# Cutting the beginning of a one-core attention block by batch and by query tile

## The chip, the core and the metric

The kernel runs on one core of a Trainium2 chip. The metric is device time in microseconds (us) of that core. Below, PE is the matrix engine (TensorE), DVE the vector engine, ACT the scalar engine, POOL the GpSimd engine and SP the engine that issues most DMAs. Each engine takes its instructions strictly in the order of its program; they meet only through semaphores.

## The reference

`x` is 2 batches of 256 tokens of 512 numbers, `ctx` 2 x 512 tokens of 128, everything float32. Three blocks follow each other, each with a residual and a layer norm:

```python
def bitnet_linear(x, weight, scale):
    s = max(mean(abs(weight), axis=1), 1e-8)
    return nan_to_num(einsum('bsi,oi->bso', x, sign(weight / s)) * (s * scale))
# 1: q = bitnet_linear(x, wq) (32 heads of 16), k, v = bitnet_linear(x, wk), (x, wv) (8 heads of 16)
#    softmax(q k / 4) v, then bitnet_linear(.., wo);       x = layernorm(x + ..)
# 2: cross attention of x on ctx, 512 keys, with an additive mask;  x = layernorm(x + ..)
# 3: y = x @ w_low.T + bias, w_low looked up in a table of 16 from 4 bit planes; x = layernorm(x + y)
```

So before the first score can be formed, the signs of the key and query weights must be multiplied with x, the absolute sums of the weights must be known, and the products scaled.

## The kernel before

**Units.** Attention is cut into 32 units: 16 of block 1 (2 batches x 8 key heads, 4 query heads each), 16 of block 2. A unit of block 1 has two key tiles (k = 0, 1), and each (unit, key tile) is a "chunk", numbered c = 2u + k. For each unit PE first forms the scores in bf16 three-part form (`scores`, L1138/L1141, into PA), DVE takes the row maxima (`maxima`, L911/L915), POOL splits these in three bf16 parts (`split_maxima`, L532 to L535), PE turns them into rows (`turn_maxima`, L1155), ACT copies the rows into QA (`rows`, L668). Only then can PE form the transposed scores with the maxima subtracted (`direct`, L1171, into PT), ACT take the exponential (`exps`, L656), and PE multiply by the values (`product`, L1199, into PO). ACT empties PO (`unload`, L675), PE turns it (`turn_unit`, L1225), DVE divides (`normalise`, L929, L934).

**Order.** All of it is written by hand. PE runs `scores` three units ahead of `direct`; `turn_maxima(u + 2)` stands at the end of chunk (u, 1), so `direct` of unit u + 1 stands behind it. `product(u)` waits for `rows(u + 2)`. POOL runs a loop over units: `split_maxima(u)`, and in units 1 to 8 two steps each of a side job `split_context` (L538 to L566): the sum of the output weights' absolute values (2 steps, in unit 1), parts of the context (8), V2 (2), and four products of the output weights with their scales `so` (2 in unit 7, 2 in unit 8). DVE has its own side job `weights` (one step in each chunk: splits of late query tiles, then bit masks and clamps, later merges), and a burst `output_scales` (L759 to L856) that forms `so`.

**Beginning.** SP loads wkv, x, wq whole, in this order. Then PE projects keys (`L1088`), queries of batch 0 (4 tiles), V (4 token tiles, L1111) and queries of batch 1 (4 tiles, L1097); a "tile" is 128 output columns. ACT scales each out of PSUM twice (L645, L646), DVE forms the bf16 parts (`split_q`, three instructions L769 to L771 behind a guard copy L800 that tests a limit read by `reg_load`), and SP spreads each part over partitions by six DMAs (`send_k`, `send_q`) into KA1 and QA, where `scores` reads them. The pairs ld_*, q_ready, q_out, q_split, qa_ready, ka1_ready are the semaphores of these steps; `signs` counts ACT's sign and absolute value of weights, `scales` DVE's scales.

**Idle products.** PE runs 28 products of constants at the start (L1084) and 28 before the last feed-forward (L1207); nothing reads them.

## Time and profile before

| | us |
|---|---|
| median of 3 runs (lowest, highest) | 313.03 (311.41, 313.76) |
| the profiled execution: its own time | 316.26 |
| the profiled execution: span of its trace | 313.5 |
| PE busy, of the span | 280.6 (89%) |
| DVE busy | 233.5 (74%) |
| ACT busy | 184.0 (59%) |
| POOL busy | 179.4 (57%) |

The span is what the trace covers; the execution's own time is 2.8 us more and lies around it. Busy time is a mean over very different stages: in the first 45 us of this program projections, splits and DMAs run, then 16 units of block 1 until about 117 us, then block 2.

### The profile page before, as it was taken

The page shows a single profiled execution, that of the slowest core. Times are in us where ns is not written, and L with a number is a line of the kernel's source. Part 1 is how long each engine was busy: PE and PEld are TensorE (multiplying, and loading weights), DVE is VectorE, ACT ScalarE, POOL GpSimd, SP SyncE. Part 2 cuts the span into 40 slices and gives each one's busy share as a digit, 9 for nine tenths or more (in the row PEclk, how much of TensorE's full clock was granted, in tenths as well). Part 3 has the DMA queues.
Part 4 walks back from the last instruction along what each step waited for, and adds up shares of the span by engine and source line. Part 5 has one row for each costly group of instructions (what it writes and reads, how often), then busy time and mean ns, then how long its engine had stood idle before and what let it go on. Part 6 is the DMA issues. An engine that isn't in the chain of part 4 may idle for free.

```text
span 313.5 us, 6246 instructions
## 1 busy us (share of the span) xinstructions
PE 280.6 (89%) x2176; PEld 176.1 (56%) x2176; DVE 233.5 (74%) x646; ACT 184.0 (59%) x325; POOL 179.4 (57%) x276
## 2 busy tenths in 40 slices
PE   7989879869898877899999899999999989999990
PEld 7679544434443332246556565666666656566880
DVE  2766377989748795997488977889899964773646
ACT  2236456867954689436456588777776754367010
POOL 8000077857975099787264897999998764320000
PEclk9979956998997997879999999999999999999997
DMA  7939942669910007600000008500000000001001
GB/s 231 365 106 124 134 45 48 90 95 205 121 53 2 0 12 125 69 2 0 4 0 2 0 17 126 64 1 2 3 0 2 1 2 0 0 36 37 0 1 67
DMA packets 15457, 17.16 MB, mean 55 GB/s; under 512 B 2112, under 2 KB 11456, under 8 KB 15424
## 3 DMA queue, kind: packets, MB, share of 16 engines
q1 hardware_dynamic: 14464, 16.29, 28.5%
...
q14 instruction: 16, 0.13, 0.2%
...
## 4 chain that ended last, share of the span: by engine, by line
PE 68%; DVE 15%; ACT 9%; issue 3%; DMA 3%; SPq 0%; POOL 0%; DVEq 0%; ACTq 0%
PE PT L1183 17%; PE PO L1199 14%; PE PA L1138 8%; DMA SM<-in_wq_T 3%; PE PT L1097 3%; PE PT L1171 3%; DVE mx L915 3%; PE PS L1237 3%; PE PA L1141 3%; ACT PTs L656 3%; PE PS L1241 2%; PE PS L1269 2%; ACT QA L668 2%; PE PT L1207 2%; PE PS L1281 2%
## 5 line engine op out<-in xcount | busy, mean ns | idle before, releaser
L656 ACT ACTIVATE PTs<-PT 128x512 f32<-128x512 f32 x192 | 110.7, 597 | 48.1 <-PE PT L1183 34.4
L596 POOL TENSOR_SCALAR SM<-SM,mx 128x512 f32<-128x512 f32 x128 | 97.3, 773 | 41.3 <-DVE mx L911 40.0
L911 DVE CUSTOM_DVE_ANT_0 SM<-PA,maskq 128x512 f32<-128x512 f32 x128 | 84.9, 685 | 20.2 <-PE PA L1138 19.9
L1183 PE MATMUL PT<-ident,SM 128*128 128x128 f32 x512 | 78.6, 278 | 2.1 <-ACT PTs L656 1.7
L1183 PEld LDWEIGHTS PT<-ident,SM 128*128 128x128 f32 x512 | 59.6, 141 | 26.2 <-issue 10.6
L1199 PE MATMUL PO<-PTs,V 128*32 128x256 f32 x768 | 54.1, 400 | 3.5 <-ACT QA L668 3.3
L1138 PE MATMUL PA<-KA,QA 96*128 96x512 bf16 x128 | 49.9, 398 | 4.7 <-DVE mx L911 4.3
L915 DVE TENSOR_REDUCE mx<-PA 128x2 f32<-128x512 f32 x64 | 40.9, 681 | 16.3 <-PE PA L1141 15.8
L1199 PEld LDWEIGHTS PO<-PTs,V 128*32 128x32 f32 x768 | 21.0, 112 | 26.2 <-issue 10.5
L532 POOL CAST SM<-mx 128x8 bf16<-128x8 f32 x16 | 5.3, 334 | 50.0 <-DVE mx L915 50.0
L1171 PE MATMUL PT<-QA,KA 99*128 99x512 bf16 x64 | 28.4, 443 | 2.5 <-ACT QA L668 1.4
L1141 PE MATMUL PA<-KA,QA 96*128 96x256 bf16 x128 | 26.6, 302 | 3.8 <-DVE mx L915 3.6
L675 ACT ACTIVATE wkvT<-PO 128x256 f32<-128x256 f32 x32 | 12.3, 384 | 24.0 <-PE PO L1199 23.9
L668 ACT ACTIVATE QA<-PO 3x512 bf16<-3x512 bf16 x32 | 18.8, 586 | 8.9 <-PE PO L1155 7.8
L1141 PEld LDWEIGHTS PA<-KA,QA 96*128 96x128 bf16 x128 | 13.0, 107 | 18.0 <-DVE mx L915 7.3
L1138 PEld LDWEIGHTS PA<-KA,QA 96*128 96x128 bf16 x128 | 12.7, 100 | 9.8 <-DVE mx L911 8.2
L583 POOL TENSOR_SCALAR wqT<-wqT,clamp_high,clamp_low 128x512 f32<-128x512 f32 x18 | 14.7, 819 | 0.8
L929 DVE RECIPROCAL rsum<-PM 128x8 f32<-128x8 f32 x32 | 6.4, 199 | 10.8 <-PE PM L1225 10.8
L1171 PEld LDWEIGHTS PT<-QA,KA 99*128 99x128 bf16 x64 | 6.7, 104 | 13.6 <-issue 7.3
L1225 PE MATMUL PM<-ident,wkvT 128*128 128x128 f32 x64 | 12.8, 282 | 0.5 <-ACT wkvT L675 0.5
L1097 PE MATMUL PT<-xT,wqT 128*128 128x256 f32 x48 | 12.7, 425 | 0.5 <-ACT wqT L632 0.5
L1097 PEld LDWEIGHTS PT<-xT,wqT 128*128 128x128 f32 x48 | 10.1, 214 | 2.3 <-ACT wqT L632 0.6
...
## 6 DMA issues: line engine op xcount, KB each, us to landing
...
```

What stands on the lines that cost most here:

```text
L583: nc.gpsimd.tensor_scalar(row, row, clamp_high[:, o, n:n + 1], clamp_low[:, o, n:n + 1], ALU.min, ALU.max).then_inc(leaf_ready, 1)
L596: nc.gpsimd.tensor_scalar(row, row, -1.0, mx[:, u % MX_RING, n:n + 1], ALU.mult, ALU.add).then_inc(sub_done, 1)
L656: nc.scalar.activation(PTs[:, c % PT_RING, j * 512:(j + 1) * 512], PT[:, (2 * c + j) % T_RING, :], ACT.Exp, scale=-1.0 if layer(u) else 1. ...
L668: nc.scalar.activation(QA[KR:KRM, b, heads.start + 2 * j:heads.start + 2 * j + 2, g * R // HT, :], maxima_rows[j], ACT.Copy).then_inc(rows ...
L911: vec.tensor_tensor_reduce(SM[:, u % SM_RING, n, :], PA[:, f % A_RING, :], maskq[:, n % QT, :], 1.0, LOWEST, ALU.add, ALU.max, mx[:, u % M ...
L915: vec.tensor_reduce(mx[:, u % MX_RING, QT * i:QT * (i + 1)], PA[:, f % A_RING, :].rearrange("p (q k) -> p q k", q=QT), AX.X, ALU.max).then ...
L1097: last = mm(q_psum(b, o), wqT[:, i, o * P:(o + 1) * P], xT[:, i, b * S:(b + 1) * S], start=(i == 0), stop=(i == DT - 1))
L1138: last = mm(PA[:, f % A_RING, :], QA[0:KR, b, h % HT, h // HT, q * P:(q + 1) * P], KA2[0:KR, g, b * T2:(b + 1) * T2], start=True, stop=True)
L1141: last = mm(PA[:, f % A_RING, q * S:(q + 1) * S], QA[0:KR, b, (g * R + i) % HT, g * R // HT, q * P:(q + 1) * P], KA1[0:KR, g, b * S:(b + 1 ...
L1171: mm(PT[:, n % T_RING, :], KA1[0:KRM, g, b * S + k * P:b * S + (k + 1) * P], QA[0:KRM, b, g * R % HT + 2 * j:g * R % HT + 2 * j + 2, g * R ...
L1183: last = nc.tensor.transpose(PT[:, n % T_RING, (i % 4) * P:(i % 4 + 1) * P], SM[:, u % SM_RING, i, k * P:(k + 1) * P], ident[:])
L1199: last = mm(PO[VW * r:VW * (r + 1), 0:S], V[:, batch(u) * key_tiles(u) + k, group(u), :], PTs[:, c % PT_RING, r * S:(r + 1) * S], start=(k ...
```

## The change

The beginning is cut finer. SP loads the first batch of x, the first quarter of wq, the second batch, the rest of wq. Keys are projected per batch; query tile (0, 0) and the keys of batch 0 are scaled, split and sent first, the tile by ACT's own DMA queue, under a limit of their own (`first_fits`). Of V, only the tiles of batch 0 stand in the beginning, behind `scores(0)`; the other two, and the query tiles (1, 2) and (1, 3), are computed by PE in the chunks 1, 2 and 4 to 7 (`later`). ACT takes the absolute value of the output weights in chunk (0, 0) and unloads the two late query tiles in chunk (4, 0). DVE's `output_scales` goes from unit 4 to unit 6, PE's sum of the output weights from unit 3 to unit 5. DVE's side job has three more steps (14 in place of 11), the split of the second batch's keys first and the split of the last two query tiles behind the clamps. Idle products go from 28 and 28 to 17 and 18. POOL's program is the same but for the counts it waits for.

```diff
-WARM = (28, 28)
+WARM = (17, 18)
...
-        OT = wkvT[:, 0, :]
+        OT = tmp2[:, 0:S]
...
+        Q_BANKS = (PT[:, 0, :], PT[:, 1, :], PO[:], PS[:])
         def q_psum(b, o):
-            bank = PS[:] if (b, o // 2) == (1, 0) else PT[:, 0 if b else o // 2, :]
-            return bank[:, (o % 2) * S:(o % 2 + 1) * S]
+            return Q_BANKS[2 * b + o // 2][:, (o % 2) * S:(o % 2 + 1) * S]
...
+        def send_q(eng, n):
+            b, o0, o1 = Q_SENDS[n]
+            eng.wait_ge(q_split, 2 + n + (n >= K_LATE))
+            for s in range(SLOTS):
+                dma_tile(eng, QA[s * HD:(s + 1) * HD, b, :, o0:o1, :], q_parts[b][:, Q_PART[s], o0:o1, :], qa_ready[n])
...
-            dma_tile(sp, xT[:], x_T.rearrange("(t p) n -> p t n", p=P), ld_x)
-            dma_tile(sp, wq_raw, wq_T.rearrange("(t p) n -> p t n", p=P), ld_wq)
+            x_rows = x_T.rearrange("(t p) n -> p t n", p=P)
+            wq_rows = wq_T.rearrange("(t p) n -> p t n", p=P)
+            dma_tile(sp, xT[:, :, 0:S], x_rows[:, :, 0:S], ld_x[0])
+            dma_tile(sp, wq_raw[:, :, 0:P], wq_rows[:, :, 0:P], ld_wq_first)
+            dma_tile(sp, xT[:, :, S:N], x_rows[:, :, S:N], ld_x[1])
+            dma_tile(sp, wq_raw[:, :, P:D], wq_rows[:, :, P:D], ld_wq_rest)
...
+            send_k(KA1[:, :, 0:S], k_parts[:, :, 0:S], ka1_ready[0])
+            for n in range(1, len(Q_SENDS)):
+                if n == K_LATE:
+                    sp.wait_ge(q_split, 2 + K_LATE)
+                    send_k(KA1[:, :, S:N], k_parts[:, :, S:N], ka1_ready[1])
+                send_q(sp, n)
...
-                pool.wait_ge(signs, 4)
+                pool.wait_ge(signs, 5)
...
-                pool.wait_ge(scales, 4)
+                pool.wait_ge(signs, 5)
+                pool.wait_ge(scales, 5)
...
-            act.wait_ge(ld_wq, 16)
-            nc.scalar.activation(wqT[:], wq_raw, ACT.Sign).then_inc(signs, 1)
-            act.wait_ge(scales, 1)
-            act.wait_ge(q_ready, 1)
-            nc.scalar.activation(k_parts[:, 0], PA[:, 0, :], ACT.Copy, scale=wsum[:, 4:5])
-            nc.scalar.activation(kf, PA[:, 0, :], ACT.Copy, scale=wsum[:, 4:5]).then_inc(q_out, 1)
-            act.wait_ge(scales, 2)
-            for b in range(B):
-                if b == 1:
-                    act.wait_ge(ld_wo, 16)
-                    link(nc.scalar.activation(woT[:], wo_raw, ACT.Sign))
-                    nc.scalar.activation(wo_raw, wo_raw, ACT.Abs).then_inc(signs, 2)
-                for o in range(DT):
-                    act.wait_ge(q_ready, 2 + b * (DT + 1) + (o | 1))
-                    nc.scalar.activation(q_parts[b][:, 0, o], q_psum(b, o), ACT.Copy, scale=wsum[:, o:o + 1])
-                    nc.scalar.activation(qf[b][:, o], q_psum(b, o), ACT.Copy,
-                                         scale=wsum[:, o:o + 1]).then_inc(q_out, 1)
+            act.wait_ge(ld_wq_first, 16)
+            nc.scalar.activation(wqT[:, :, 0:P], wq_raw[:, :, 0:P], ACT.Sign).then_inc(signs, 1)
+            def unload_k(b):
+                act.wait_ge(q_ready, 1 + 2 * b)
+                act.wait_ge(scales, 1)
+                nc.scalar.activation(k_parts[:, 0, b * S:(b + 1) * S], PA[:, b, 0:S], ACT.Copy, scale=wsum[:, DT:DT + 1])
+                nc.scalar.activation(kf[:, b * S:(b + 1) * S], PA[:, b, 0:S], ACT.Copy, scale=wsum[:, DT:DT + 1]).then_inc(q_out, 1)
+            def unload_q(b, o, ready):
+                act.wait_ge(q_ready, ready)
+                act.wait_ge(scales, 3 if b or o else 2)
+                nc.scalar.activation(q_parts[b][:, 0, o], q_psum(b, o), ACT.Copy, scale=wsum[:, o:o + 1])
+                nc.scalar.activation(qf[b][:, o], q_psum(b, o), ACT.Copy, scale=wsum[:, o:o + 1]).then_inc(q_out, 1)
+            unload_k(0)
+            act.wait_ge(ld_wq_rest, 16)
+            nc.scalar.activation(wqT[:, :, P:D], wq_raw[:, :, P:D], ACT.Sign).then_inc(signs, 1)
+            unload_q(0, 0, 2)
+            unload_k(1)
+            send_q(act, 0)
+            act.wait_ge(ld_wo, 16)
+            link(nc.scalar.activation(woT[:], wo_raw, ACT.Sign))
+            unload_q(0, 1, 4)
+            unload_q(0, 2, 6)
+            unload_q(0, 3, 6)
+            unload_q(1, 0, 8)
+            unload_q(1, 1, 8)
...
+                    if (u, k) == (0, 0):
+                        nc.scalar.activation(wo_raw, wo_raw, ACT.Abs).then_inc(signs, 2)
+                    if (u, k) == (4, 0):
+                        unload_q(1, 2, 4 + B * DT)
+                        unload_q(1, 3, 4 + B * DT)
...
+            dve.wait_ge(ld_x[0], 16)
+            vec.tensor_reduce(bound[:, 0:1], xT[:, :, 0:S], AX.XY, ALU.max, apply_absolute_value=True)
+            dve.wait_ge(ld_wq_first, 16)
+            link(vec.tensor_reduce(abs_q[:, 0:P], wq_raw[:, :, 0:P].rearrange("p i o -> p o i"), AX.X, ALU.add, apply_absolute_value=True))
+            def scale(total, given, extra, out_):
+                link(vec.tensor_scalar(out_, total, 1.0 / D, 1e-8, ALU.mult, ALU.max))
+                return vec.scalar_tensor_tensor(out=out_, in0=out_, scalar=extra, in1=given, op0=ALU.mult, op1=ALU.mult)
+            dve.wait_ge(ld_scl, 16)
+            dve.wait_ge(sums_ready, 1)
+            scale(PM[:, DT:DT + 1], scl[:, DT:DT + 1], 1.0, wsum[:, DT:DT + 1]).then_inc(scales, 1)
+            vec.tensor_reduce(bound[:, 1:2], abs_q[:, 0:P], AX.X, ALU.add).then_inc(abs_ready, 1)
...
+            dve.wait_ge(sums_ready, 2)
+            plus_one(0, 4)
+            scale(PM[:, 0:1], scl[:, 0:1], HD ** -0.5, wsum[:, 0:1]).then_inc(scales, 1)
+            link(vec.tensor_scalar(all_w, w_first, w_kv, all_scl, ALU.add, ALU.mult))
+            link(vec.tensor_scalar(fits[:, 0:1], all_w, x_first, SAFE / D, ALU.mult, ALU.is_lt))
+            first_fits, qkv_fits, o_fits = dve.alloc_register("first_fits"), dve.alloc_register("qkv_fits"), dve.alloc_register("o_fits")
+            dve.reg_load(first_fits, fits[0:1, 0:1])
+            finish(split_k(0))
+            finish(split_q(0))
+            dve.wait_ge(ld_wq_rest, 16)
+            link(vec.tensor_reduce(abs_q[:, P:D], wq_raw[:, :, P:D].rearrange("p i o -> p o i"), AX.X, ALU.add, apply_absolute_value=True))
+            dve.wait_ge(ld_x[1], 16)
+            vec.tensor_reduce(bound[:, 4:5], xT[:, :, S:N], AX.XY, ALU.max, apply_absolute_value=True)
+            vec.tensor_reduce(bound[:, 5:6], abs_q[:, P:D], AX.X, ALU.add).then_inc(abs_ready, 1)
+            dve.wait_ge(ld_scales, 16 * 2)
+            link(vec.tensor_reduce(all_s, vo_scales[:, 0:KV], AX.X, ALU.add, apply_absolute_value=True))
+            dve.wait_ge(sums_ready, 3)
+            plus_one(4, 6)
+            scale(PM[:, 1:DT], scl[:, 1:DT], HD ** -0.5, wsum[:, 1:DT]).then_inc(scales, 1)
+            link(vec.tensor_scalar(all_w, w_first, w_kv, w_rest, ALU.add, ALU.add))
+            link(vec.tensor_tensor(all_s, all_s, all_scl, ALU.add))
+            link(vec.tensor_scalar(all_x, x_first, x_rest, all_s, ALU.add, ALU.mult))
+            link(vec.scalar_tensor_tensor(out=most, in0=all_w, scalar=float(D), in1=all_x, op0=ALU.mult, op1=ALU.mult))
+            link(vec.tensor_scalar(fits[:, 1:2], most, SAFE, None, ALU.is_lt))
+            dve.reg_load(qkv_fits, fits[0:1, 1:2])
+            finish(split_q(1))
+            def values(b):
+                if b == 0:
+                    link(scale(PM[:, P:P + KV], vo_scales[:, 0:KV], 1.0, sv))
+                    dve.wait_ge(const_ready, 2)
+                dve.wait_ge(q_ready, 9 + b)
+                for t in range(b * QT, (b + 1) * QT):
+                    vec.tensor_tensor(V1[:, t, :, 0:HD], PS[:, t * KV:(t + 1) * KV].rearrange("p (g d) -> p g d", g=G),
+                                      sv.rearrange("p (g d) -> p g d", g=G), ALU.mult).then_inc(v_out, 1)
+                dve.wait_ge(v_out, (b + 1) * QT)
+                guard(qkv_fits, HUGE, *[V1[:, t, :, 0:HD] for t in range(b * QT, (b + 1) * QT)])
...
+                yield from split_k(1)
+                yield from split_q(3)
...
-            for u in range(SCORES_FIRST):
-                for i in range(fills(u)):
-                    maxima(u, i)
+            for i in range(fills(0)):
+                maxima(0, i)
+            finish(split_q(2))
+            for i in range(fills(1)):
+                maxima(1, i)
+            values(0)
             for u in range(UNITS):
                 ahead = upcoming(u)
-                if u == 4:
+                if u == 6:
                     output_scales()
                 for k in range(key_tiles(u)):
                     for v, i in ahead[k * len(ahead) // key_tiles(u):(k + 1) * len(ahead) // key_tiles(u)]:
                         maxima(v, i)
                     now[0] = first_chunk(u) + k
+                    if now[0] == 3:
+                        values(1)
...
+            def project_k(b):
+                pe.wait_ge(ld_x[b], 16)
+                for i in range(DT):
+                    last = mm(PA[:, b, 0:S], wkvT[:, i, 0:KV], xT[:, i, b * S:(b + 1) * S], start=(i == 0), stop=(i == DT - 1))
+                last.then_inc(q_ready, 1)
+            def project_q(b, o, tiles=range(DT)):
+                for i in tiles:
+                    last = mm(q_psum(b, o), wqT[:, i, o * P:(o + 1) * P], xT[:, i, b * S:(b + 1) * S],
+                              start=(i == 0), stop=(i == DT - 1))
+                if DT - 1 in tiles:
+                    last.then_inc(q_ready, 1)
+            def project_v(t):
+                for i in range(DT):
+                    last = mm(PS[:, t * KV:(t + 1) * KV], xT[:, i, t * P:(t + 1) * P], wkvT[:, i, KV:2 * KV],
+                              start=(i == 0), stop=(i == DT - 1))
+                if t % QT == QT - 1:
+                    last.then_inc(q_ready, 1)
+            def later(c):
+                if c in (1, 2):
+                    if c == 1:
+                        pe.wait_ge(v_out, QT)
+                    project_v(QT + c - 1)
+                if 4 <= c <= 7:
+                    if c == 4:
+                        pe.wait_ge(v_out, NT)
+                    project_q(1, 2 + (c - 4) // 2, range((c - 4) % 2 * 2, (c - 4) % 2 * 2 + 2))
+            project_k(0)
+            pe.wait_ge(scales, 1)
+            sums(PM[:, 0:1], abs_q[:, 0:P], 1, 2)
+            mm(PM[:, B_COL:B_COL + 4], ones[:], bound[:, 0:4], start=True, stop=True).then_inc(sums_ready, 1)
+            project_q(0, 0)
+            project_k(1)
+            pe.wait_ge(signs, 3)
+            pe.wait_ge(q_out, 2)
+            for o in range(1, DT):
+                project_q(0, o)
+            pe.wait_ge(scales, 2)
+            for o in range(1, DT):
+                sums(PM[:, o:o + 1], abs_q[:, o * P:(o + 1) * P], 1, 3)
+            mm(PM[:, B_COL + 4:B_COL + 6], ones[:], bound[:, 4:6], start=True, stop=True).then_inc(sums_ready, 1)
+            project_q(1, 0)
+            project_q(1, 1)
...
                 scores(0, i)
+            for t in range(QT):
+                project_v(t)
+            turn_maxima(0)
             for i in range(fills(1)):
                 scores(1, i)
...
-                    if u == 3 and k == 0:
-                        pe.wait_ge(q_out, 1 + B * DT)
+                    later(first_chunk(u) + k)
+                    if u == 5 and k == 0:
+                        pe.wait_ge(q_out, 2 + B * DT)
```

On ACT, around its first units (L645/L646 and L658/L659 scale query tiles; QA is `rows`, PTs `exps`, `SM 128x2048` is the absolute value of the output weights), before:

```order
L645 ACTIVATE O<-PT,wsum 128x256
L646 ACTIVATE SM<-PT,wsum 128x256
L641 ACTIVATE woT<-SM 128x2048
L642 ACTIVATE SM<-SM 128x2048
L645 ACTIVATE x<-PS,wsum 128x256
L646 ACTIVATE SM<-PS,wsum 128x256
```

and with the change:

```order
L694 ACTIVATE QA<-PO 3x2x256 x2
L682 ACTIVATE PTs<-PT 128x512 x2
L694 ACTIVATE QA<-PO 3x2x256 x2
L742 ACTIVATE SM<-SM 128x2048
L682 ACTIVATE PTs<-PT 128x512 x2
L694 ACTIVATE QA<-PO 3x2x256 x2
```

The absolute value stood before the scaling of batch 1's tiles; it now stands behind `rows(1)`, the second QA row.

On PE, in units 0 and 1 with the change (L1240 is `turn_maxima`, L1256 `direct`, L1226 `scores`, L1284 `product`, L1164 one V tile):

```order
L1256 MATMUL PT<-QA,KA 128x512
L1226 MATMUL PA<-KA,QA 128x256 x4
L1164 MATMUL PS<-wkvT,xT 128x128 x4
L1240 MATMUL PO<-SM 3x128 x8
L1256 MATMUL PT<-QA,KA 128x512
L1226 MATMUL PA<-KA,QA 128x256 x2
L1256 MATMUL PT<-QA,KA 128x512
L1226 MATMUL PA<-KA,QA 128x256 x2
L1284 MATMUL PO<-PTs,V 32x256 x8
L1164 MATMUL PS<-wkvT,xT 128x128 x4
```

Both L1164 rows are new there; `turn_maxima(2)`, the L1240 row, and `direct(1, 0)` behind it stand as before.

On DVE, the burst `output_scales`, before (in unit 4) and with the change (in unit 6, behind the first step of the last query split, L797):

```order
L864 TENSOR_SCALAR masks<-planes 128x256 x2
L759 TENSOR_SCALAR tmp<-PS 128x512
L760 SCALAR_TENSOR_TENSOR tmp<-tmp,maskq 128x512
L851 TENSOR_REDUCE limit<-tmp 128x1
L852 TENSOR_SCALAR limit<-limit 128x1
L853 TENSOR_TENSOR limit<-limit 128x1
L854 TENSOR_SCALAR fits<-limit 128x1
L856 TENSOR_LOAD fits
L915 TENSOR_REDUCE mx<-PA 128x2 x2
```

```order
L797 TENSOR_TENSOR SM<-SM,x 128x2x256
L785 TENSOR_SCALAR tmp<-PS 128x512
L786 SCALAR_TENSOR_TENSOR tmp<-tmp,maskq 128x512
L907 TENSOR_REDUCE product_of<-tmp 128x1
L908 TENSOR_SCALAR product_of<-product_of 128x1
L909 TENSOR_TENSOR product_of<-product_of 128x1
L910 TENSOR_SCALAR fits<-product_of 128x1
L912 TENSOR_LOAD fits
L972 TENSOR_REDUCE mx<-PA 128x2 x2
```

What reads `so` did not move. On POOL with the change, units 7 and 8 of its loop:

```order
L544 CAST SM<-mx 128x4x2
L545 TENSOR_TENSOR mx_left<-mx,SM 128x8
L546 CAST SM<-mx_left 128x4x2
L547 TENSOR_TENSOR SM<-mx_left,SM 128x4x2
L578 TENSOR_TENSOR woT<-woT,tmp 128x512 x2
L544 CAST SM<-mx 128x4x2
```

The L578 row waits for DVE's burst, and `split_maxima(8)`, whose first row is the last one, stands behind it.

## Rows read from the trace of the kernel before

**Rows 1.** The chain of waits, 0 to 90 us: start, us, what.

```profile
18.41 6.97 PE PT L1097 x24
25.38 3.57 PE PO L1111 x32
...
32.41 3.45 PE PT L1097 x16
```

**Rows 2.** Timeline of DVE in the beginning: start, us, what, idle before it.

```profile
8.67 2.29 DVE L748 TENSOR_REDUCE bound<-xT 128x1 f32<-128x2048 f32 x1 [1.82 <-DMA xT<-in_x_T]
...
12.29 3.74 DVE L752 TENSOR_REDUCE SM<-SM 128x512 f32<-128x2048 f32 x1 [1.01 <-DMA SM<-in_wq_T]
...
20.98 0.14 DVE L800 COPY guard_tmp<-ident 1x1 f32<-1x1 f32 x1 [1.02 <-issue]
...
23.01 0.14 DVE L800 COPY guard_tmp<-ident 1x1 f32<-1x1 f32 x1
...
24.32 0.13 DVE L800 COPY guard_tmp<-ident 1x1 f32<-1x1 f32 x1
```

**Rows 3.** Timeline of SP, sends of batch 0's query tiles.

```profile
27.00 11.55 SPq L447 DMA_DIRECT2D QA<-O  x18
```

**Rows 4.** Page, part 6: DMA issues, KB each, us to landing.

```profile
QA<-O SPq DMA_DIRECT2D x12, 64.0 KB, 4.3
```

**Rows 5.** Timeline of PE: scores(2), then the first direct of units 1, 2, 4, 6, 7.

```profile
42.28 1.06 PE L1141 MATMUL PA<-KA,QA 96*128 96x256 bf16 x4
...
48.29 0.61 PE L1171 MATMUL PT<-QA,KA 99*128 99x512 bf16 x1
...
54.05 0.39 PE L1171 MATMUL PT<-QA,KA 99*128 99x512 bf16 x1
...
63.01 0.39 PE L1171 MATMUL PT<-QA,KA 99*128 99x512 bf16 x1
...
74.50 0.39 PE L1171 MATMUL PT<-QA,KA 99*128 99x512 bf16 x1
...
78.52 0.39 PE L1171 MATMUL PT<-QA,KA 99*128 99x512 bf16 x1
```

**Rows 6.** Timeline of ACT: output weights' absolute value, one query tile, rows(1).

```profile
28.88 1.91 ACT L642 ACTIVATE SM<-SM 128x2048 f32<-128x2048 f32 x1
...
32.45 0.47 ACT L645 ACTIVATE x<-PS,wsum 128x256 bf16<-128x256 f32 x1 [1.65 <-PE PS L1097]
...
45.21 1.20 ACT L668 ACTIVATE QA<-PO 3x512 bf16<-3x512 bf16 x2 [0.81 <-PE PO L1155]
```

**Rows 7.** Timeline of POOL: weights' sums, last step of split_maxima(2), output weights scaled.

```profile
42.16 2.35 POOL L540 TENSOR_TENSOR SM<-SM 128x1024 f32<-128x1024 f32 x1
44.59 1.27 POOL L542 TENSOR_TENSOR SM<-SM 128x512 f32<-128x512 f32 x1
...
47.13 0.23 POOL L535 TENSOR_TENSOR SM<-mx_left,SM 128x8 bf16<-128x8 f32 x1
...
71.94 2.49 POOL L565 TENSOR_TENSOR woT<-woT,tmp 128x512 f32<-128x512 f32 x2
```

**Rows 8.** Timeline of DVE: first and last arithmetic of output_scales.

```profile
64.22 0.68 DVE L759 TENSOR_SCALAR tmp<-PS 128x512 f32<-128x512 f32 x1
...
66.83 0.15 DVE L854 TENSOR_SCALAR fits<-limit 128x1 int32<-128x1 f32 x1
```

**Rows 9.** Stretches of PE: us, busy (instructions), granted clock, DMA share, GB/s.

```profile
36.00:42.00 6.00, 3.28 (x24) 0.79 1.14 128
42.00:53.00 11.00, 11.00 (x62) 0.50 0.03 6
...
70.00:73.50 3.50, 3.19 (x22) 0.53 0.93 315
```

**Rows 10.** The chain of waits at the end.

```profile
291.83 6.25 PE PT L1207 x56
```

**Rows 11.** Timeline of DVE at the end: batch 1's last tiles of x2.

```profile
295.97 1.00 DVE L977 TENSOR_SCALAR x<-woT,mv,root 128x512 f32<-128x512 f32 x2
```

143 lines of the change are left out of this document (45 added, 98 removed).

## The prediction

> **What bounds the kernel now.** I read the chain of waits first, then the timeline of each engine around the pieces that the change moves, then the stretches with the granted clock. In the chain the first thing to see is that PE is continuously on it from 18.4 to 35.9 us [rows 1]: three query tiles, four V tiles (3.57), four query tiles, of which the last two take 3.45. Only behind them come scores and maxima, and PE reaches `scores(2)` at 42.28 [rows 5]. That beginning is what the change cuts.
>
> The second thing is the loop of the units. From `direct` of unit 6 to that of unit 7 it is 78.52 - 74.50 = 4.0 us [rows 5], the steady length: `product`, `direct` and `scores` of the second key tile, `turn_maxima`, ACT's `rows` (1.20 [rows 6]), next `product`. PE and ACT are both on it, so anything put into it on either lengthens it. Units 4 and 5 take 11.5 together, 3.5 too much: DVE's burst stands there [rows 8], 64.22 to 66.98. Third, the clock: 42 to 53 us ran at 0.50 of full speed, i.e. at 1.2 GHz, behind a stretch in which PE had work for 3.28 of 6 us [rows 9].
>
> The fourth is POOL. The sums of the output weights (2.35 and 1.27) and `split_maxima(2)` follow on each other, 42.16 to 47.36, 5.2 us [rows 7], and PE, 1 us later at `direct(1)`, just doesn't feel it.
>
> **The change, part by part.**
>
> *Beginning, -8.5.* x came at 8.67 and wq at 12.29 [rows 2], 3.6 us a megabyte. Half of x then lands at about 6.9, the first quarter of wq at 7.8. DVE takes the limit of half of x (2.29/2 = 1.15) and the sums of a quarter of the weights (3.74/4 = 0.94), until 9.0. From the end of the sums to the guard before, scales, limits and register read took 20.98 - 16.03 = 4.95 [rows 2]; with one column instead of four I take 4.9, so 13.9. Keys and tile (0, 0), 256 columns each, cost 1.3 each (24.32 - 23.01 [rows 2]): 16.5. Then the rest of the weights (2.8), the other half of x (1.15), the same block again (4.95) and tile (0, 1) (1.3): 26.7; part of the small limits falls beside PE's work, I take 26.3. SP issues six sends at 11.55/18 = 0.64 [rows 3], the last 3.2 later, and it lands after 4.3 [rows 4]: 33.8. PE has by then done keys, six query tiles and `scores(0)`, `scores(1)`: its projections end at about 25.4 (five tiles of 1.73 from 11.4, two key halves of 1.8, the second sums at 21.8). So `scores(2)` waits for tile (0, 1) and starts at 33.8 against 42.28: 8.5 us gained. The bounds are 31.9, when `rows(0)` alone releases PE, and 35.5, if loads or sends take a fifth longer.
>
> *POOL in unit 0, +5.8.* POOL's sums of the output weights wait for ACT's absolute value, which was done at 30.8 and now stands behind `rows(1)`. From `scores(2)` to the end of `rows(1)` it was 46.41 - 42.28 = 4.1 [rows 5, 6], so `rows(1)` ends at 37.9, the absolute value (1.91 [rows 6]) at 39.8, and POOL's 5.2 us [rows 7] at 45.0. `turn_maxima(2)` stands behind `split_maxima(2)`, `direct(1)` behind it: 45.6 against 48.29. Without the wait it would be 39.8. PE stands for nearly 5 us; the V tile of chunk 1 is hidden there and costs nothing. If the cover went, it would cost 0.9. Of 8.5 us 2.7 are left.
>
> *Projections in the loop, +4.9.* The V tile of chunk 2 costs 3.57/4 = 0.9 at full clock, 1.8 at half; I take 1.4. Four halves of query tiles cost 0.86 each [rows 1], 3.5. All stand between two `product`s or before `turn_maxima`, on the loop.
>
> *ACT in unit 4, +1.6.* Four scalings of 0.47 [rows 6], a little overlapped. They stand between `unload` and the second `exps`, before `rows(6)`.
>
> *DVE's burst, -3.5 and +4.6.* Leaving unit 4 it gives back the 3.5 us of units 4 and 5. The sum on PE (L1315) only changes units, 0. In unit 6 the burst has a new waiter: POOL asks for `so` in its own unit 7, and `split_maxima(8)` stands behind. DVE begins the burst 1.2 us after `direct` of the unit (64.22 - 63.01 [rows 5, 8]), 0.4 more for the split step ahead, and signals 2.8 later: 4.4. POOL's two products take 2.49 [rows 7], `split_maxima(8)` 1.3 (between 1.1 and the 1.5 from 45.86 to 47.36), `turn_maxima(8)` 0.4: unit 7 begins 8.6 us after unit 6 and not 4.0. Bounds: 3, if DVE is a unit's slack ahead, and 6.
>
> *Clock behind that stop, +1.7.* After the shorter stop of the old burst 70 to 73.5 ran at 0.53 [rows 9]: 3.5 us at half speed lose 1.7. In unit 1 I leave the old length, 5.8 [rows 5], which is already at half clock.
>
> *Splits of query tiles (1, 2), (1, 3).* Their last step comes about 9.5 us after unit 6 begins, the sends land 8 us later, when unit 9 asks for them, 17.5 after unit 6. I take 0, bound +1.
>
> *Idle products, -1.4.* The last 28 take 6.25 us and end at 298.08 [rows 10], 0.223 each; 18 end at 295.9. x2 of the first tile was ready at about 296.6 [rows 11]. So the tail moves by 298.0 - 296.6 = 1.4, and DVE is next. At the start 17 end at 6.7, before x is there: 0, the load covers it; without the cut they would cost 3.
>
> Sum: -8.5 + 5.8 + 4.9 + 1.6 - 3.5 + 4.6 + 1.7 - 1.4 = **+5.2 us**. Durations are from the execution of 316.26 us, span 313.5, which lies 1% above the median of 313.03; I put the difference on the median: **318.2**.
>
> On the clock, row and rule part: here PE was busy for all of 42 to 53 us and still had 0.50 [rows 9]. The Trainium skill, "TensorE: Matmul & The Clock Gate", section "What's actually happening", says that the default is the throttled state and activity releases it. By that, unit 1, with a V tile more and few waits, would come back to 2.4 GHz early: 0.5 less for the V tile, some 1.8 less in unit 1, and the sum would be +2.9. The long slow stretch speaks against it, so it has a chance of its own below.
>
> **Rivals.**
>
> *Slower by little or not at all, the clock comes back early (0.1).* With activity behind the stop of unit 0, unit 1 takes 4.0 and not 5.8, the V tile 0.9: 5.2 - 2.3 = +2.9, 315.9. For it: 70 to 73.5 was short [rows 9]; against it: 42 to 53 was not.
>
> *POOL's waits don't bite (0.12).* If the absolute value or the burst came early enough, 5.8 and 4.6 + 1.7 fall away. Left are the 1.9 of ACT before the second `exps`, 0.9 for the first V tile, and a burst on DVE as costly as before (3.5): 5.2 - 12.1 + 6.3 = -0.6, 312.4. Against it stands only the order of the programs, which is strict.
>
> *Faster (0.1).* One place decides: `direct(1)`. If it starts before about 41 us, PE never stands long in units 0 and 1, and the slow stretch of 42 to 53 goes as well: 54.05 - 42.28 = 11.8 us for what takes 8 at full clock, 3.8 us. From -0.6 this leads to -4.4, 308.6.
>
> *Much slower (0.13).* The low clock lasts through units 2 and 3 too, as 11 us of it did before; the query halves cost twice (+3.5) and the late tiles hold unit 9 (+1): +9.7, 322.9.
>
> *Forecast (0.55)*: both POOL waits hold PE. Its own range is 315.9 to 320.5, from the bounds of the start of `scores(2)` (-1.9, +1.7) and of the second stop (-1.6, +1.4), not all at one end.
>
> **Numbers.** About 1%, 3.1 us, is what a measurement can tell from no change. Faster by more: the faster rival and a tail of the second, 0.12. Within: the early clock, most of the second rival, a sliver of the forecast, 0.25. Slower: most of the forecast and the last rival, 0.63. The range 311.8 to 322.0 leaves out the faster rival and most of the slowest.
>
> **What would show it.** The first `scores(2)` at 32 to 35.5 us. On POOL an idle time of some 4 us before the sums, put down to ACT, and PE idle for some 5 us before `turn_maxima(2)`; `direct(1)` at 44 to 47. Units 2 and 3 of 5.7 us or more, unit 4 about 5.6, unit 5 about 5. In unit 6 POOL waiting for DVE before L578 and 8 to 9 us to unit 7. The last idle products end before x2 is ready. I am wrong if POOL doesn't wait at those two places, or if the moved projections fall into waits of PE.

## The result and the profile after

The changed kernel takes 321.48 us (median of 4 runs, 319.33 to 324.26), against 313.39 for the kernel before on the same chip: ratio 1.0236, 95% interval [1.0137, 1.0335]. The ratio leaves out the execution of 324.26, which was in a slower state; the medians by themselves give 1.026. It is slower, as forecast; 321.5 lies inside the range, 3.3 us above the predicted 318.2, but above the 315.9 to 320.5 that the forecast gave for its own case. The profiled execution took 319.33 us, span 317.5.

PE is busy 7.5 us less than before, DVE 3.9 more, ACT and POOL as before: the loss is not more work but waiting, with stretches at half clock. From the page of the changed kernel:

```profile
span 317.5 us, 6222 instructions
PE 273.1 (86%) x2144; PEld 173.1 (55%) x2144; DVE 237.4 (75%) x658; ACT 184.0 (58%) x328; POOL 179.6 (57%) x276
```

The start of the first `direct` of each unit, read from PE's timeline, is the ruler for everything below; a unit "takes" the time from its start to the next unit's (us; "shift" is after minus before):

| unit | 0 | 1 | 2 | 3 | 4 | 5 | 6 | 7 | 8 | 9 |
|---|---|---|---|---|---|---|---|---|---|---|
| before | 41.91 | 48.29 | 54.05 | 58.05 | 63.01 | 69.08 | 74.50 | 78.52 | 82.52 | 86.52 |
| after | 33.12 | 46.17 | 53.17 | 58.99 | 64.82 | 69.80 | 76.72 | 85.96 | 90.94 | 94.94 |
| shift | -8.8 | -2.1 | -0.9 | +0.9 | +1.8 | +0.7 | +2.2 | +7.4 | +8.4 | +8.4 |

8.8 us are won by unit 0, 6.7 of them are gone by unit 1, and the rest and 8.4 more by unit 8. PE's timeline shows both places (start, duration, line, what; in brackets the idle time before and who ended it):

```profile
33.52 0.90 PE L1226 MATMUL PA<-KA,QA 96*128 96x256 bf16 x4
36.87 0.39 PE L1226 MATMUL PA<-KA,QA 96*128 96x256 bf16 x2 [1.86 <-DVE mx L972]
...
40.17 1.92 PE L1164 MATMUL PS<-wkvT,xT 128*128 128x128 f32 x8
45.64 0.60 PE L1240 MATMUL PO<-SM 128*3 128x128 bf16 x8 [3.55 <-POOL SM L547]
46.17 0.61 PE L1256 MATMUL PT<-QA,KA 99*128 99x512 bf16 x1
...
55.64 1.13 PE L1156 MATMUL PS<-xT,wqT 128*128 128x256 f32 x4
...
69.80 0.39 PE L1256 MATMUL PT<-QA,KA 99*128 99x512 bf16 x1 [0.91 <-ACT PTs L682]
...
71.59 1.56 PE L1284 MATMUL PO<-PTs,V 128*32 128x256 f32 x16 [0.70 <-ACT QA L694]
73.08 2.08 PE L1403 MATMUL PS<-SM,ones 128*128 128x512 f32 x2
...
82.71 0.61 PE L1226 MATMUL PA<-KA,QA 96*128 96x256 bf16 x2 [2.69 <-DVE mx L972]
...
85.42 0.60 PE L1240 MATMUL PO<-SM 128*3 128x128 bf16 x8 [1.68 <-POOL SM L547]
85.96 0.61 PE L1256 MATMUL PT<-QA,KA 99*128 99x512 bf16 x1
```

Against [rows 5]: `scores(2)` starts at 33.52 and not 42.28. PE then stands 3.55 us for POOL in unit 0, and in unit 6 first 2.69 us for DVE and then 1.68 us for POOL. Who holds POOL in unit 0 stands on ACT and POOL, the rows that answer to [rows 6, 7]:

```profile
37.65 1.20 ACT L694 ACTIVATE QA<-PO 3x512 bf16<-3x512 bf16 x2 [2.38 <-PE PO L1240]
38.88 1.91 ACT L742 ACTIVATE SM<-SM 128x2048 f32<-128x2048 f32 x1
```

```profile
40.86 2.35 POOL L552 TENSOR_TENSOR SM<-SM 128x1024 f32<-128x1024 f32 x1 [5.11 <-ACT SM L742]
43.29 1.26 POOL L554 TENSOR_TENSOR SM<-SM 128x512 f32<-128x512 f32 x1
...
45.36 0.23 POOL L547 TENSOR_TENSOR SM<-mx_left,SM 128x8 bf16<-128x8 f32 x1
...
81.65 2.48 POOL L578 TENSOR_TENSOR woT<-woT,tmp 128x512 f32<-128x512 f32 x2 [10.81 <-DVE fits L910]
```

The last row is the second stop: POOL waited for the end of DVE's burst. Read with it the clock of PE's stretches (us, busy with instructions, granted clock, DMA share, GB/s), beside [rows 9]:

```profile
38.00:52.00 14.00, 10.20 (x58) 0.52 0.07 16
52.00:70.00 18.00, 15.84 (x147) 1.00 0.37 57
72.00:75.00 3.00, 3.00 (x18) 0.51 0.00 0
78.00:82.00 4.00, 1.83 (x20) 1.00 0.00 2
82.00:90.00 8.00, 5.61 (x38) 0.57 0.17 39
```

About half of full speed (1.2 GHz) from 38 to 52, 72 to 75 and 82 to 89. In the fourth row PE is busy 1.83 of 4 us at full clock, and the fall comes behind it.

### The profile page after: what moved, and what is told of

It reads as the page before. It is cut to its first block, busy times and chain, and to the rows that moved or that the text cites. A ratio compares the mean times of both kernels' runs of the same rounds, so it can differ in the third digit from the quotient of the medians.

```text
span 317.5 us, 6222 instructions
## 1 busy us (share of the span) xinstructions
PE 273.1 (86%) x2144; PEld 173.1 (55%) x2144; DVE 237.4 (75%) x658; ACT 184.0 (58%) x328; POOL 179.6 (57%) x276
## 4 chain that ended last, share of the span: by engine, by line
PE 59%; DVE 18%; ACT 10%; issue 6%; POOL 3%; DMA 2%; DVEq 1%; SPq 0%; POOLq 0%; ACTq 0%
PE PT L1268 16%; PE PO L1284 14%; PE PA L1223 7%; ACT PTs L682 3%; DVE SM L968 3%; DVE mx L972 3%; ACT QA L694 3%; PE PT L1256 2%; PE PS L1322 2%; DMA SM<-in_wq_T 2%; PE PS L1326 2%; PE PS L1354 2%; PE PA L1226 2%; PE PS L1366 2%; PE PM L1310 2%
## 5 line engine op out<-in xcount | busy, mean ns | idle before, releaser
L1284 PE MATMUL PO<-PTs,V 128*32 128x256 f32 x768 | 53.7, 397 | 3.9 <-ACT QA L694 3.7
L1223 PE MATMUL PA<-KA,QA 96*128 96x512 bf16 x128 | 49.1, 390 | 5.5 <-DVE mx L968 5.3
L1284 PEld LDWEIGHTS PO<-PTs,V 128*32 128x32 f32 x768 | 20.9, 111 | 26.0 <-issue 10.9
L1226 PE MATMUL PA<-KA,QA 96*128 96x256 bf16 x128 | 25.8, 292 | 6.3 <-DVE mx L972 5.8
L1256 PE MATMUL PT<-QA,KA 99*128 99x512 bf16 x64 | 26.5, 414 | 2.3 <-ACT PTs L682 2.3
L701 ACT ACTIVATE tmp<-PO 128x256 f32<-128x256 f32 x32 | 12.3, 384 | 23.2 <-PE PO L1284 23.0
L1226 PEld LDWEIGHTS PA<-KA,QA 96*128 96x128 bf16 x128 | 12.1, 103 | 20.2 <-DVE mx L972 9.7
L1223 PEld LDWEIGHTS PA<-KA,QA 96*128 96x128 bf16 x128 | 12.6, 99 | 10.3 <-DVE mx L968 9.3
L1310 PE MATMUL PM<-ident,tmp 128*128 128x128 f32 x64 | 12.9, 283 | 0.5 <-ACT tmp L701 0.5
L1240 PE MATMUL PO<-SM 128*3 128x128 bf16 x128 | 6.8, 230 | 6.9 <-POOL SM L547 6.9
L1256 PEld LDWEIGHTS PT<-QA,KA 99*128 99x128 bf16 x64 | 6.5, 101 | 10.8 <-ACT PTs L682 5.3
L578 POOL TENSOR_TENSOR woT<-woT,tmp 128x512 f32<-128x512 f32 x4 | 5.4, 1376 | 10.8 <-DVE fits L910 10.8
```

Of the source, the lines that this page charges most:

```text
L1223: last = mm(PA[:, f % A_RING, :], QA[0:KR, b, h % HT, h // HT, q * P:(q + 1) * P], KA2[0:KR, g, b * T2:(b + 1) * T2], start=True, stop=True)
L1226: last = mm(PA[:, f % A_RING, q * S:(q + 1) * S], QA[0:KR, b, (g * R + i) % HT, g * R // HT, q * P:(q + 1) * P], KA1[0:KR, g, b * S:(b + 1 ...
L1256: mm(PT[:, n % T_RING, :], KA1[0:KRM, g, b * S + k * P:b * S + (k + 1) * P], QA[0:KRM, b, g * R % HT + 2 * j:g * R % HT + 2 * j + 2, g * R ...
L1284: last = mm(PO[VW * r:VW * (r + 1), 0:S], V[:, batch(u) * key_tiles(u) + k, group(u), :], PTs[:, c % PT_RING, r * S:(r + 1) * S], start=(k ...
L1310: last = nc.tensor.transpose(PM[:, q * P:(q + 1) * P], OT[:, q * P:(q + 1) * P], ident[:])
```

## The experiments

Twelve kernels, each timed beside the kernel before on the same chip. Between executions of one kernel the time varies by 1 to 2%, together with the mean granted clock (0.93 to 0.97). So I read mechanisms from the unit starts, and sizes from medians and ratios; where these differ, both are given.

**First series: the two POOL waits.** The weights' absolute value put back early on ACT, in the changed kernel:

```
             unload_q(1, 1, 8)
+            nc.scalar.activation(wo_raw, wo_raw, ACT.Abs).then_inc(signs, 2)
...
-                    if (u, k) == (0, 0):
-                        nc.scalar.activation(wo_raw, wo_raw, ACT.Abs).then_inc(signs, 2)
```

> The changed kernel with the output weights' absolute value on ACT behind the unloading of query tile (1, 1), where ACT stands idle from 28.0 to 31.8 us, instead of behind rows(1). Theory (POOL's wait for it holds PE): POOL starts its sums right behind split_maxima(1), at about 36, turn_maxima(2) comes at about 41.5 instead of 45.6 and direct(1) at 42 instead of 46.2; the span is 3 to 6 us shorter than the changed kernel's, 312 to 314. Rival (the moved projections and the low clock are what costs, POOL's wait only lies beside it): direct(1) moves by less than 1.5 us, span 316 or more.

Measured: 315.36 us (ratio 1.0089, [1.0043, 1.0135]), span 313.8. Units 1, 2 and 9 begin at 43.58, 48.56 and 89.97. PE:

```profile
41.20 1.92 PE L1163 MATMUL PS<-wkvT,xT 128*128 128x128 f32 x8
43.05 0.60 PE L1239 MATMUL PO<-SM 128*3 128x128 bf16 x8
43.58 0.61 PE L1255 MATMUL PT<-QA,KA 99*128 99x512 bf16 x1
```

The POOL wait is gone: no idle time stands before the turn of the maxima. `direct(1)` gains 2.6 us and not the whole 3.55 of the wait, because the V tile itself begins 1.0 us later here (41.20 for 40.17): unit 0 began 0.5 later, and the clock was low (0.55) from 34 to 38 us already, where the changed kernel had 0.99. The V tile, which lay under POOL's delay before, is now part of what PE has to do there, at half clock (1.92). Unit 2 begins 4.6 us earlier, since the clock is back within unit 1 (1.00 from 45 us; in the changed kernel unit 1 runs at half clock until 51.6).

The reverse, in the kernel before: the absolute value moved behind `rows(1)` of unit 0.

```
-                    nc.scalar.activation(wo_raw, wo_raw, ACT.Abs).then_inc(signs, 2)
...
+                    if (u, k) == (0, 0):
+                        nc.scalar.activation(wo_raw, wo_raw, ACT.Abs).then_inc(signs, 2)
```

> The kernel before with nothing changed but the place of the output weights' absolute value on ACT: behind rows(1) in chunk (0, 0). Theory: rows(1) ends at 46.4, the absolute value at 48.3, POOL's sums and split_maxima(2) 5.2 later, so direct(1) comes at about 54 instead of 48.3 and the kernel is 4 to 6 us slower, 317 to 319. Rival (POOL's wait lies beside PE's low clock): slower by 0 to 2 us.

Measured: 318.88 us (6.0 above the median of before; ratio 1.0137, [1.0061, 1.0214], which is 4.3), unit 1 at 54.22 (48.29 before), 5.9 us later. One instruction of 1.91 us, moved by itself, stops PE for 5.42 us:

```profile
53.68 0.60 PE L1156 MATMUL PO<-SM 128*3 128x128 bf16 x8 [5.42 <-POOL SM L535]
```

The second wait: POOL's scaling of the output weights, two products per unit of its loop, one unit later.

```
-                for _ in range(2 * (1 <= u <= 8)):
+                for _ in range(2 * (1 <= u <= 9 and u != 7)):
```

> The changed kernel with POOL's four products of the output weights in units 8 and 9 of its loop (two each, behind split_maxima(8) and split_maxima(9)) instead of 7 and 8. Theory: split_maxima(8) no longer waits for DVE's burst; unit 6 takes 5 to 7 us instead of 9.2 (DVE's burst itself still delays the maxima of unit 9), and the slow-clock stretch behind it shrinks; span 3 to 5 us shorter, about 313.5. Rival (DVE's burst and split alone hold PE in unit 6): unit 6 stays above 8 us, span 316 or more.

Measured: 319.18 us (ratio 1.0139, [1.006, 1.0218]), span 319.0: neither the 5 to 7 us for unit 6 nor the shorter span came. Unit 6 takes 7.48 us and not 9.24, unit 7 5.92 and not 4.98. PE, where POOL no longer holds it:

```profile
83.82 0.61 PE L1226 MATMUL PA<-KA,QA 96*128 96x256 bf16 x2 [2.67 <-DVE mx L972]
...
84.79 0.60 PE L1240 MATMUL PO<-SM 128*3 128x128 bf16 x8
```

The wait for DVE's maxima, 2.67 us, is untouched: it is the burst itself. POOL's part of unit 6 is 1.8 us, and half of it comes back in unit 7. I had put the whole stop down to POOL.

The burst and PE's sum for it moved to units 6 and 5 in the kernel before:

```
-                if u == 4:
+                if u == 6:
                     output_scales()
...
-                    if u == 3 and k == 0:
+                    if u == 5 and k == 0:
```

> The kernel before with DVE's burst output_scales in unit 6 and PE's sum of the output weights in unit 5, nothing else. Theory: units 4 and 5 give back some 3 us, unit 6 takes 8 to 9 instead of 4.0 because POOL waits before split_maxima(8), and a low-clock stretch follows; net 1 to 4 us slower, 314 to 317. Rival (the burst costs the same wherever it stands): within 1 us of before, unit 6 at 6 us or less.

Measured: 314.99 us (ratio 1.0079, [1.0034, 1.0124]). Units 2, 3 and 4 take 4.00 each, unit 5 5.39, unit 6 7.92 (PE stands 2.19 us for DVE's maxima and 1.49 for POOL), unit 7 5.10. Units 4 and 5 take 9.4 together and not 8, because PE's sum now stands in unit 5. It costs 1.4 there and cost 1.0 in unit 3, which took 4.96. Units 3 to 5 together fall from 16.45 to 13.39 us: with the 0.4 that the sum costs more, the burst had cost 3.5 in its old place.

**Second series: do the parts add up, and what of the rest.** Both cures together:

> The changed kernel with both cures of the GpSimd waits: the weights' abs as early as in the kernel before, and GpSimd's scaling of the output weights in units 8 and 9. My theory (the three causes add up: abs behind unit 0, GpSimd waiting for fits, DVE's burst in unit 6): first direct of unit 1 at 43.6, of unit 6 at about 70.5, unit 6 itself 7.5 us as when the scaling alone was moved, so unit 9 begins at about 88 (94.94 in the changed kernel, 89.97 with the early abs alone), span 312 to 313, median 313 to 315. Rival (unit 6 is limited by DVE's burst whatever GpSimd does, the gain of the later scaling is given back in unit 7): unit 9 at 89.5 to 90.5, no better than the early abs alone.

Measured: 313.89 us (ratio 1.0039, [1.0, 1.0078]), span 312.8. Units 1, 6, 7 and 9 begin at 43.86, 72.39, 79.88 and 90.08. The median is where the theory had it, the unit starts are where the rival had them: unit 9 no earlier than with the first cure alone. In this profile unit 5 ran in a low clock (6.92), with the first cure alone it did not (5.29). Against the kernel before, 8.1 us in the medians become 1.1 with both orders of POOL changed; the unit starts show less of it, 4.9 of the 8.4 us at unit 9. Most of it is the first cure: the second takes the loss from 2.5 to 1.1 us, and the two intervals overlap.

On top of both cures, DVE's scales cut into four pieces (a `yield` behind each) that stand behind the maxima:

```
-                if u == 6:
-                    output_scales()
...
                         maxima(v, i)
+                    if u in (6, 7):
+                        next(scales_work, None)
```

> As the run before, and DVE's output scales are cut into four pieces, one behind the row maxima of each key tile of units 6 and 7, and not one burst of 2.8 us ahead of them. My theory (the burst stands ahead of the maxima for which PE waits, and the stop it makes lowers the clock): PE's wait of 2.7 us for the maxima in unit 6 goes, the granted clock stays at 1.00 there, units 6 and 7 take 8 to 9.5 us together and not 12.5 to 14, unit 9 begins at about 84 to 85, and the median is 309 to 312, at or below the kernel before. Rival (DVE is simply full in these units, so that the same work cut up gives the same delay): units 6 and 7 take 12 us or more, unit 9 at 88 or later, median 313 to 315.

Measured: 317.56 us (ratio 1.0156, [1.0102, 1.0209]). Unit 6 is a clean 4.00 us, PE's longest wait in it 0.41. But the pieces end at 82.56, and POOL's scaling waited for them ahead of the next shares. PE, then POOL:

```profile
79.82 0.38 PE L1313 MATMUL PM<-ident,tmp 128*128 128x128 f32 x2
86.28 0.60 PE L1243 MATMUL PO<-SM 128*3 128x128 bf16 x8 [6.08 <-POOL SM L547]
```

```profile
82.70 2.48 POOL L578 TENSOR_TENSOR woT<-woT,tmp 128x512 f32<-128x512 f32 x2 [9.51 <-DVE fits L912]
85.13 0.22 POOL L544 CAST SM<-mx 128x8 bf16<-128x8 f32 x1
```

My theory was right on DVE and forgot POOL: the same strict order, one unit on, and a stop of 6.08 us, the longest of all. So POOL's scaling one more unit later:

```
-                for _ in range(2 * (1 <= u <= 9 and u != 7)):
+                for _ in range(2 * (1 <= u <= 6 or u in (9, 10))):
```

> The kernel with the pieces of the output scales behind the maxima, and GpSimd's scaling of the output weights moved on by one more unit of its loop (9 and 10), since the pieces end at 82.4 us and GpSimd waited for them ahead of the shares of unit 8. My theory (with that wait gone nothing stops PE in units 6 to 8, and the clock stays at 1.00): unit 6 begins at 71.6 and takes 4.0 us as in the run before, unit 7 4.5 to 5 us, unit 9 begins at 84.5 to 87 (90.08 with both cures alone, 86.52 in the kernel before), no PE wait above 1 us between 70 and 88 us; median 309.5 to 312.5, at or under the kernel before. Rival (GpSimd, now 5 us of work behind, holds the shares of unit 10 or its clamps, or the maxima are late in the next unit): a wait of 2 us or more on GpSimd's shares turns up between 84 and 95 us, and the median is 314 or more.

Measured: 315.62 us (ratio 1.0074, [1.0038, 1.011]). Units 6, 7, 8 and 9 begin at 72.06, 76.06, 80.90 and 87.27, with PE waits of 0.72 and 1.20 us in unit 8; unit 9, which took 9.7 before, takes 14.2. The long waits are gone as in my theory, the gain in the median is not: it is where the rival had it. With ACT's two unloads split over unit 4 as well (`if u == 4: unload_q(1, 2 + k, ...)` in place of both at k = 0):

> As the run before, with ScalarE's two late unloads in the two key tiles of unit 4. My theory: units 4 and 5 take 4.3 and 5.3 us as they did when this alone was changed (unit 4 was 4.25 and not 4.98), so unit 6 begins 0.7 us earlier than in the run before and the median is 0.5 to 1 us lower. Rival: the freed time is waited out in the next unit, no difference beyond 0.3 us in the profile and none in the median.

Measured: 314.06 us (ratio 1.0035, [0.9993, 1.0078]). Unit 6 begins at 69.86 and unit 9 at 84.88, ahead of the kernel before (86.52); unit 10 at 97.52, behind it (96.23). Unit 9 takes 12.6 us. POOL's last two products, then PE's first output projection:

```profile
88.17 2.49 POOL L578 TENSOR_TENSOR woT<-woT,tmp 128x512 f32<-128x512 f32 x2
```

```profile
90.76 1.96 PE L1324 MATMUL PS<-woT,oT 128*128 128x512 f32 x4 [1.09 <-issue]
```

The projection needs all four scaled tiles and starts 0.1 us behind them. This PE wait of 1.09, one of 0.53 at 85.80 for the late query tile, whose last part landed at 85.7, and a new stretch of half clock (0.50 from 86 to 88 us) take back what units 6 to 8 gave. None of the three places tried for the scaling was free: too early it waits for the scales, too late PE waits for it. Spreading it over more units was not tried.

The unload split alone, in the changed kernel:

> The changed kernel with ScalarE's two late unloads put into different key tiles of unit 4, 0.95 us in each, and not both into the first. My theory (both together hold the score tiles back by 1.9 us, PE then stands 0.9 and 0.7 us and its clock falls at 71.6): PE's waits of 0.91 at 69.80 and 0.70 at 71.59 shrink to under 0.4 each, the clock stays at 1.00 from 70 to 75, unit 5 takes 5 to 5.6 us and not 6.92, and unit 6 begins at about 75.5 and not 76.72. Rival (ScalarE is full in units 4 and 5 and loses the same 1.9 us anyway, the clock falls for another reason): unit 5 stays at 6.5 to 7 us, or unit 4 takes up what unit 5 gives.

Measured: 320.46 us (ratio 1.0240, [1.0179, 1.0301]), no gain beyond the scatter. Unit 4 takes 4.25 and not 4.98, and unit 5 5.28 with the clock at 1.00. That looks like the theory, but it is not shown: with the early absolute value and with the spread scales unit 5 took 5.29 and 5.28 too, with both unloads still in one key tile and the old waits unchanged. From the spread kernel:

```profile
66.34 0.39 PE L1259 MATMUL PT<-QA,KA 99*128 99x512 bf16 x1 [0.91 <-ACT PTs L683]
...
68.13 1.07 PE L1287 MATMUL PO<-PTs,V 128*32 128x256 f32 x16 [0.70 <-ACT QA L695]
```

The same waits of 0.91 and 0.70 led to a low clock in some executions and to none in others. ACT's two unloads cost unit 4 1.0 us (4.98 for 4.0), of which the split saves 0.7; the 1.6 in unit 5 is the clock's.

Six of the eight late query products left out, so that this kernel does not compute those queries:

```
-                    project_q(1, 2 + (c - 4) // 2, range((c - 4) % 2 * 2, (c - 4) % 2 * 2 + 2))
+                    if c % 2:
+                        o = 2 + (c - 4) // 2
+                        mm(q_psum(1, o), wqT[:, 3, o * P:(o + 1) * P], xT[:, 3, S:2 * S], start=True, stop=True).then_inc(q_ready, 1)
```

> The changed kernel leaving out 6 of the 8 products of the two late query tiles (that part of batch 1's queries isn't computed); their unloads stay. My theory (PE is the limit in units 2 and 3, so the halves cost there what they last, 0.87 us each): units 2 and 3 take about 4.5 us each and not 5.82 and 5.83, unit 4 begins at 62.2 to 62.4 and not 64.82; the unload in unit 4 costs as before. Rival (the halves fill time in which PE would wait for ScalarE's score tiles): units 2 and 3 stay above 5.3 us, unit 4 at 64 or later.

Measured: 318.95 us (ratio 1.0198, [1.0147, 1.025]). Unit 3 takes 4.43 and not 5.83, as the theory had it. Unit 2 takes 5.16 and not 5.82, since PE now stands 0.56 us there for DVE's maxima. Unit 4 begins 15.73 us behind unit 1, not 18.65; of these 2.9 us 2.1 are won in units 2 and 3, and the rest in unit 1, where the clock came back sooner. So the halves are paid in full in unit 3, and about half of them in unit 2. At its place unit 4 begins at 63.29, 0.9 later than I wrote, because unit 1 began at 47.56 in this execution.

**Third series: the idle products.** In the kernel before, 18 for 28 at the end:

```
-WARM = (28, 28)
+WARM = (28, 18)
```

> The kernel before with 18 idle products in place of 28 ahead of its last phase, as the change has it, and nothing else. My theory (the time of ten idle products, 1.3 us, is taken out of PE's queue at the end, since the transposes behind them stand 1.4 us behind their data): the last phase of PE (feed-forward products) begins 1.2 to 1.5 us sooner behind the last turn of a unit, and the median falls by 1.0 to 1.5 us, to 0.995 to 0.997 of the kernel before. Rival (x1 and its transposes wait for DVE or ScalarE, or the clock falls for want of the idle products): no gain, or slower by 1 us and more, PE waiting for DVE there and a granted clock of 0.5 in the last 10 us.

Measured: 310.98 us against 313.06. PE's tail, beside [rows 10]:

```profile
287.52 0.44 PE L1225 MATMUL PM<-ident,wkvT 128*128 128x128 f32 x2 [0.50 <-ACT wkvT L675]
287.79 4.18 PE L1207 MATMUL PT<-ident,ones 128*128 128x128 f32 x36
292.71 0.66 PE L1281 MATMUL PS<-ident,x 128*128 128x128 f32 x4 [0.73 <-DVE x L977]
...
294.05 3.72 PE L1265 MATMUL PA<-wqT,oT 128*128 128x256 f32 x16 [0.23 <-ACT oT L686]
```

From the last turn of a unit to the feed-forward products it is 6.53 us and was 7.82 (291.39 to 299.21): 1.29 gained, DVE next, as the prediction had it. With 17 at the start as well, `WARM = (17, 18)`:

> The kernel before with both numbers of idle products as the change has them, 17 at the start and 18 at the end, and nothing else. My theory (at the start the data cover the idle products, so 11 fewer cost and gain nothing; at the end they are worth 1.3 us): the first scores(2) of the unit loop begins within 0.5 us of where it does with 28 at the start (40.8 to 42.3), the tail as with 18 at the end alone, the median 310.5 to 312.5, 0.993 to 0.997 of the kernel before. Rival one (the idle products at the start, which ended at 9.76 us and were followed by the key product at once, held it): scores(2) begins 1 us or more sooner. Rival two (without them the clock falls in the first 12 us): the key product or the query tiles run at half speed, scores(2) later by 1 us or more.

Measured: 310.49 against 313.63. `scores(2)` starts at 42.40 (42.28 before): the start is worth nothing. The key product came 1.1 us sooner (8.62 for 9.76) and PE waited for ACT's signs of the query weights 1.63 us and not 0.45. This profile ran the tail as the one above, 6.53 us.

These two kernels are faster than both given ones. The ratios, 0.9888 [0.9846, 0.993] and 0.9863 [0.9811, 0.9915], overstate the gain, because they do not compare executions at the same clock. Sorted by mean granted clock, those with 0.95 or more have medians of 310.23 and 310.25 against 312.55 and 313.07, those under 0.95 313.88 and 314.35 (one run) against 315.54 and 315.32. So the gain is 1 to 3 us. The trace shows 1.3 of it; where the rest would come from stays open.

## Why the prediction was right

The sign was right for the reasons given, and its largest term, POOL's order behind a moved ACT instruction, is shown from both sides. Cured, it takes the loss against the kernel before from 8.1 to 2.5 us in the medians (by the ratios from 7.4 to 2.8); made alone in the kernel before, it costs 6.0 (4.3). The size was less right: +5.2 was forecast for the sum, and +8.1 was measured. Term by term:

| term | forecast | measured |
|---|---|---|
| `scores(2)` | -8.5 (33.8) | -8.8 (33.52) |
| `direct(1)` | 45.6 | 46.17 |
| V tile in unit 1 | +1.4 | +1.2 (unit 7.00, was 5.76) |
| query halves, units 2, 3 | +3.5 | +2.7 (11.65, were 8.96) |
| units 4, 5: ACT +1.6, burst gone -3.5 | -1.9 | +0.4 (11.90, were 11.49) |
| unit 6, burst and POOL | +4.6 | +5.2 (9.24, was 4.02) |
| clock behind it | +1.7 | +1.0 (unit 7 4.98) |
| late query tiles in unit 9 | 0 (bound +1) | 0 (9.72, was 9.71; PE waits 0.36 for them) |
| idle products at the end | -1.4 | -1.3 (6.53 from the last turn of a unit to the feed-forward products, was 7.82) |

*Beginning.* The start of `scores(2)` came within 0.3, but by luck. First, a step in the sum was off: the first quarter of the query weights came at 9.50 and not 7.8. DVE shows it:

```profile
9.50 1.05 DVE L781 TENSOR_REDUCE SM<-SM 128x128 f32<-128x512 f32 x1 [1.41 <-DMA SM<-in_wq_T]
```

The guard of the keys came at 14.25 (forecast 13.9): from the end of the sums, 10.55, the small steps took 3.7 us and not the 4.9 allowed, which covered most of the error. Second, what released PE was not what the prediction said. ACT and SP:

```profile
31.78 1.20 ACT L694 ACTIVATE QA<-PO 3x512 bf16<-3x512 bf16 x2 [3.73 <-PE PO L1240]
```

```profile
26.61 8.38 SPq L452 DMA_DIRECT2D QA<-O  x12
```

The first six of these sends are tile (0, 1); the sixth went out at 29.77 and landed at 32.2, 2.4 us later and not 4.3. So the tile was there before `rows(0)` ended, at 32.98. Then came `direct(0)` at 33.12 and `scores(2)` at 33.52, with no idle time of PE between them. `rows(0)` alone released PE: that is the case which the prediction gave as its lower bound, 31.9, and it came 1.6 later. Third, the 17 idle products ended at 8.34 and not at 6.7, behind the first half of x, which DVE read from 6.87 on. So they held PE's first key product; nothing shows that this cost time, since the next steps waited for the weights of 9.50.

*Query halves.* Each takes 0.86 to 0.97 (forecast 0.86), and units 2 and 3 take 3.65 us more than two units of 4.0. The term comes out smaller against before because unit 3 of before already held PE's sum for the burst (4.96, not 4.0).

*Units 4 and 5, the term that failed.* It was 2.3 us too low. The -3.5 for the burst was right, as moving only the burst and the sum shows. What came in its place was not. PE's sum costs 1.3 in unit 5 (5.28 for 4.0), and it gave back 1.0 in unit 3, which is in the row above. So "only changes units, 0" was 0.3 too low, and it is the rows on units 2 to 5 together that can be compared: +1.6 forecast, +3.1 measured. ACT's unloads cost 1.0 and not 1.6. And unit 5 fell into a low clock, 6.92 for the 5.28 of other kernels' profiles: 1.6 us that the forecast had nowhere, and the rest of the difference.

*Unit 6.* The size was nearly right, the mechanism half right. The prediction let POOL's order make the whole stop. Moved away, it gives 1.8 of 5.2; the burst itself, between PE's scores and the maxima that release it, makes the other 3.5 (2.67 of it is PE's wait for the maxima, much of the rest the half clock behind it). The rows of before had shown that. In unit 4 PE stood 1.90 us for DVE's maxima behind the burst, with no wait for POOL, and units 4 and 5 took 3.5 us too long:

```profile
68.20 0.39 PE L1141 MATMUL PA<-KA,QA 96*128 96x256 bf16 x2 [1.90 <-DVE mx L915]
```

*The median.* The trace gives +8.4 at unit 9 and -1.3 at the end, +7.1, and the medians +8.1 to +8.4. The two spans differ by 4.0 only, since the profiled execution of before had low clocks later on that the one of after lacked (0.74 and 1.00 for 120 to 140 us). Putting the sum on the median of 313.03 was the right choice, as 313.39 this time shows; on the profiled 316.26 it would have given 321.5, the measured time, by luck. The miss lies in the sum, +5.2 for +8.1. The trace accounts for 1.9 us of it: units 2 to 5 (1.5), `direct(1)` (0.6) and unit 6 (0.6), less 0.7 for the clock behind it and 0.1 for the rest. The last microsecond, between +7.1 in the traces and +8.1 in the medians, stays open.

*The rivals.* That POOL's waits don't bite would have given 312.4; the kernel that makes them not bite, with all else changed, has 313.9. The clock did not come back early: half speed held from 38 to 52 us, through a stop and 10.20 us of work. Units 2 and 3 ran at 1.00, so the much slower rival fell too, although its 322.9 (its own terms add up to 322.7) lies nearer to the measured 321.5 than the forecast does: the time alone would have picked the wrong case. The Trainium skill, "TensorE: Matmul & The Clock Gate", section "What's actually happening", has activity release the throttled state; in each case the clock did come back while PE worked without a stop, but not at once: in the changed kernel at 51.6 us, behind work from 45.64 on, on [rows 9] behind 11.00 us of work, and with the early absolute value at about 44.6, behind work from 37.38 on.
